# Two exponentials taken from tanh: (1+t)/(1-t) with the quotient on VectorE

## The reference

```python
x = x + conv_ref(ln_c(x), ...)      # deformable convolution, 8 groups, 9 taps
t = t + ffn_ref(ln_t(t), ...)       # 8 experts, the best two of each token
# conv_ref
x1 = gelu(layernorm(depthwise3x3(inputs) + dw_bias))
offset = (x1 @ w_off + b_off).reshape(B, H, W, G, K2, 2)
mask = softmax((x1 @ w_mask + b_mask).reshape(B, H, W, G, K2), axis=-1)
out = sum over the taps of bilinear_sample(x @ w_in + b_in, offset) * mask
return out @ w_out + b_out
# ffn_ref
probs = softmax(xt @ Wr + br); top_p, top_idx = top_k(probs, 2)
weights = top_p / top_p.sum(-1)
y = gelu(layernorm(xt) @ W1[e] + b1[e]) @ W2[e] + b2[e], weighted sum of the two
```

## Time and profile before

| | us |
|---|---|
| median of 3 runs (lowest, highest) | 315.28 (314.25, 315.37) |
| span of the profiled execution, first to last instruction | 312.6 |
| TensorE busy | 278.6 (89%) |
| ScalarE busy | 257.1 (82%) |
| VectorE busy | 240.5 (77%) |
| GpSimd busy | 122.1 (39%) |

### The profile page before, as it was taken

How to read it: one execution, slowest core, us unless ns; L and a number is a source line. 1 busy time by engine, 2 the same in 40 slices (tenths; PEclk the granted TensorE clock), 3 DMA queues, 4 the chain that set the end, 5 groups by cost and what they waited for, 6 DMA issues and landing times.

```text
span 312.6 us, 8542 instructions
## 1 busy us (share of the span) xinstructions
PE 278.6 (89%) x3312; PEld 179.4 (57%) x3312; DVE 240.5 (77%) x720; ACT 257.1 (82%) x495; POOL 122.1 (39%) x123
## 2 busy tenths in 40 slices
PE   7977898968799998899999997999979999998895
PEld 2552476635467654445667663444667787776562
DVE  6999769999957987679878887498958354479565
ACT  3878679899796999989796999988868899887473
POOL 5230151504452705031584413050966713569230
PEclk9999999999999999999999999999999999999999
DMA  6910000000000000000000000000000000000000
GB/s 143 306 37 0 3 2 4 0 2 2 0 3 2 4 2 0 2 0 3 2 9 13 2 0 0 3 2 1 2 19 0 3 2 2 10 1 12 2 0 17
DMA packets 7189, 4.84 MB, mean 15 GB/s; under 512 B 5089, under 2 KB 6830, under 8 KB 7086
## 3 DMA queue, kind: packets, MB, share of 16 engines
q1 hardware_dynamic: 7150, 4.31, 5.7%
HBM read 2.04 MB, written 0.52 MB: 8 GB/s over the span
## 4 chain that ended last, share of the span: by engine, by line
PE 43%; DVE 23%; ACT 18%; issue 9%; POOL 6%; DMA 1%; DVEq 0%; ACTq 0%; POOLq 0%
ACT wk L1284 5%; PE zl_ps L1533 5%; ACT wk L1279 4%; PE ga_ps L1564 3%; PE zh_ps L1530 3%; PE m_ps L1666 3%; PE ga_ps L1566 3%; PE ga_ps L1565 3%; DVE wx L851 3%; DVE prod L863 3%; PE m_ps L1649 2%; ACT h_all L1315 2%; PE m_ps L1507 2%; DVE samp L878 2%; PE m_ps L1452 2%
## 5 line engine op out<-in xcount | busy, mean ns | idle before, releaser
L863 DVE TENSOR_TENSOR prod<-ga_ps,wx 128x480 f32<-128x480 f32 x96 | 61.9, 651 | 30.3 <-PE ga_ps L1566 29.5
L547 POOL TENSOR_TENSOR prod<-prod 128x960 f32<-128x960 f32 (+1 forms) x20 | 39.8, 1991 | 111.6 <-DVE prod L863 111.6
L1279 ACT ACTIVATE wk<-zh_ps 128x512 f16<-128x512 f32 x108 | 65.3, 604 | 21.7 <-PE zh_ps L1530 20.6
L1564 PE MATMUL ga_ps<-v_all,wk 128*128 128x80 f16 x576 | 79.2, 201 | 4.0 <-DVE prod L863 1.4
L1566 PE MATMUL ga_ps<-v_all,wk 128*128 128x80 f16 x576 | 79.2, 202 | 0.0
L1565 PE MATMUL ga_ps<-v_all,wk 128*128 128x80 f16 x576 | 79.1, 201 | 0.0
L1564 PEld LDWEIGHTS ga_ps<-v_all,wk 128*128 128x128 f16 x576 | 56.5, 98 | 17.1 <-issue 6.3
L1284 ACT ACTIVATE wk<-zl_ps 128x512 f16<-128x512 f32 x108 | 65.6, 607 | 0.0
L1565 PEld LDWEIGHTS ga_ps<-v_all,wk 128*128 128x128 f16 x576 | 57.0, 99 | 7.8
L1566 PEld LDWEIGHTS ga_ps<-v_all,wk 128*128 128x128 f16 x576 | 57.2, 99 | 0.0
L1533 PE MATMUL zl_ps<-tab,sel_lo 128*128 128x512 f16 x108 | 41.6, 385 | 7.0 <-ACT wk L1284 4.4
(11 more groups left out here) (283 smaller groups left out, 622.2 us busy)
## 6 DMA issues: line engine op xcount, KB each, us to landing
v_all<-still SPq DMA_DIRECT2D x1, 1440.0 KB, 9.9
h_all<-in_W SPq DMA_DIRECT2D x1, 512.0 KB
w_s<-in_W SPq DMA_DIRECT2D x1, 512.0 KB
x_tok<-in_x SPq DMA_DIRECT2D x1, 384.0 KB, 6.4
out_dram<-x_tok SPq DMA_DIRECT2D x6, 64.0 KB, 1.7
w_high<-w_high SPq DMA_DIRECT2D x1, 256.0 KB, 2.9
const<-in_table SPq DMA_DIRECT2D x1, 218.0 KB, 2.6
vec<-in_vectors SPq DMA_DIRECT2D x1, 132.5 KB
```

Of the source, the lines that this page charges most:

```text
L547: then(pool.tensor_tensor(p[:, 0:3, :], p[:, 0:3, :], p[:, 3:6, :], ALU.add))
L863: dve.tensor_tensor(prod[q % 2][:].rearrange("p k n -> p (k n)")[:, f * PB * NV:(f + 1) * PB * NV] .rearrange("p (n c l) -> p n c l", n=PB ...
L1279: act.activation(wk[n % WR][:, 0, :], zh_ps[:], ACT.Relu, scale=W_SCALE).then_inc(s_wkh, 1)
L1564: pe.matmul(to, w_h, high, start=True, stop=False)
```

## The change

`tap_exp` and `router_exp` on ScalarE take tanh of half the argument, and VectorE computes (1 + t) / (1 - t) in three linked instructions: 1 - t, its reciprocal, and (t + 1) times that. The quotient equals exp of the argument. The three stand at the head of `tap_weights`, for all four chunks, on 128 x 288, and at the head of `expert_weights` for chunks 0 and 1, on 128 x 32. The router of chunks 2 and 3 stays on GpSimd. The warm-up with Exp is gone.

```diff
@@ tap_weights (VectorE)
                 dve.wait_ge(s_ex, a + 1)
                 dve.wait_ge(s_chain, seen["edge"])
+                link(dve.tensor_scalar(below_one[:], th[:], -1.0, 1.0, ALU.mult, ALU.add))
+                link(dve.reciprocal(below_one[:], below_one[:]))
+                link(dve.scalar_tensor_tensor(ex[:], th[:], 1.0, below_one[:], ALU.add, ALU.mult))
@@ expert_weights (VectorE)
                 dve.wait_ge(s_chain, seen["top"])
+                if d < LAST - 1:
+                    link(dve.tensor_scalar(le_below[:], le_th[:], -1.0, 1.0, ALU.mult, ALU.add))
+                    link(dve.reciprocal(le_below[:], le_below[:]))
+                    link(dve.scalar_tensor_tensor(lx[:], le_th[:], 1.0, le_below[:], ALU.add, ALU.mult))
@@ tap_exp (ScalarE)
-                act.activation(ex[:], es[:], ACT.Exp).then_inc(s_ex, 1)
+                act.activation(th[:], es[:], ACT.Tanh, scale=0.5).then_inc(s_ex, 1)
@@ router_exp (ScalarE)
-                act.activation(lx[:, t, :], le[:, t, :], ACT.Exp).then_inc(s_lx, 1)
+                act.activation(le_th[:, t, :], le[:, t, :], ACT.Tanh, scale=0.5).then_inc(s_lx, 1)
@@ before body 0 (ScalarE)
-            act.activation(warm[:, 1:2], still[:, 0:1], ACT.Exp)
```

More of the change, by code:

```diff
@@ L295, in build @@
         mx = sb("mx", [P, TP, Q, 2])
-        warm = sb("warm", [P, 2])
+        warm = sb("warm", [P, 1])
         es = sb("es", [P, TP * S])
         ex = sb("ex", [P, TP * S])
+        th = sb("th", [P, TP * S])
+        below_one = sb("below_one", [P, TP * S])
+        le_th = sb("le_th", [P, TP, E])
+        le_below = sb("le_below", [P, TP, E])
         mask = sb("mask", [P, TP * S])
```

## The result

The changed kernel takes 327.45 us (median of 4 runs, 326.84 to 328.03) against 314.79 us (4 runs, 314.25 to 315.37). The ratio is 1.039, with a 95% interval of 1.036 to 1.042. The forecast was 319.6 us, with a range of 315.0 to 322.5. The sign was right and the time lies 5 us above the range. The profiled execution took 328.02 us, with a span of 326.0 us against 312.6 before.

What follows compares the result with a forecast made beforehand. No engine is full; the chain passes between TensorE, VectorE and ScalarE. Terms 2.83 + 2.73 - 1.1 - 0.2 = +4.3 us on the 315.28 us median gave 319.6 us, range 315.0 to 322.5.

Steps and rivals of the forecast that it cites:

- The price of the passes: Three linked VectorE passes over 128x288 cost 2.83 us a block, with the reciprocal at 1.95 us.
- The table loads: On ScalarE, eight of ten activation-table loads go, leaving two, both at the start.
- Chunk 0 and body 0: VectorE's block stands in the open or in a full stretch: +2.83 us, then +2.83 less 0.1.
- (c): Rival: TensorE's clock falls to 1.2 GHz after the wait before `xn`, 1 to 14 us, taken as 3: 322.6 us; chance 0.08.
- The wait before `xn`: TensorE's wait near the start grows from 0.83 to 3.66 us.
- The warm-up load: Load at 20.8 us, ahead of the chain on VectorE, which does not wait for ScalarE there: worth 0.
- Body 1: ScalarE gives 3.04 us, the block costs 2.83, `feat` had 0.95 of slack: net -1.1 us.
- The loads at 120.9 and 188.3 us lie full on the chain: 1.42 each: In chunks 1 and 2, removing each of these ScalarE loads gains its whole 1.42 us.
- The first load: Load at 109.6 us, priced by its twin without it one chunk later: worth 0.77 us.
- Body 2: ScalarE gives 2.27 us, the block costs 2.83, 0.77 of pause precedes the product at 218.36 us: net -0.2 us.
- (a): Rival: VectorE's block is hidden in bodies 1 and 2 and all ScalarE's gain arrives: +0.25, 315.5 us; chance 0.17.

Runs made afterwards that it cites:

- keep_start: Changed kernel plus 17 matmuls of zeros ahead of TensorE's wait for `xn` of chunk 1; 322.31 us, ratio 1.024.
- two_zeros: Changed kernel plus 2 matmuls of zeros ahead of TensorE's wait for `xn` of chunk 1; 325.75 us, ratio 1.034.
- no_passes: Changed kernel without the VectorE quotients, tanh written where the exponential stood, so the weights are no exponentials; 312.89 us, ratio 0.992.
- delay_start_plus: Kernel before plus unread VectorE pass, reciprocal and two plain passes over 128x288, ahead of chunk 0's weights alone; 323.26 us, ratio 1.021.
- delay_start_double: Kernel before plus unread VectorE passes over 128x288 with two reciprocals, ahead of chunk 0's weights alone; 324.05 us, ratio 1.024.
- pool_newton: Exp kept for chunks 0 and 1; chunks 2 and 3 take tanh with the quotient on GpSimd by Newton steps; 312.94 us, ratio 0.993 against the kernel before.
- exp_first_two: Exp kept for chunks 0 and 1; chunks 2 and 3 take tanh with the quotient on VectorE; 319.14 us, ratio 1.011 against the kernel before.

## Why the prediction was wrong, point by point

The span grew by 13.4 us where 4.3 were summed. Of the 9.1 us between them 6.6 are TensorE's clock, which the sum has at nothing, and 2.5 are ScalarE's gain, which it has too large.

- **The price of the passes: right.** 2.83 us a block was forecast and 2.82 is what each adds between `hats` and `esum`. The slope through two small reciprocals held: 1953 ns against 1.95 us. The Trainium skill ("VectorE: DVE Perf Modes", First, the fixed hardware budget) gives a repeat count of 8 for the divide. The trace disagrees with the estimate of 8.3 ns an element made from it: (1953 - 178) / 284 is 6.25 ns.
- **The table loads: right.** Two are left. The row for GELU of the Trainium skill ("ScalarE: Activation LUTs", Table sets: the hidden batching unit) does not list tanh. The trace goes against keeping the two apart: tanh and GELU alternate there with no load between them.
- **Chunk 0 and body 0, taken as delay: right.** Forecast +2.83 and +2.73, and `keep_start` shows +2.73 and +2.76.
- **The step that failed most: the sum has nothing for the clock, and (c) was mis-weighed.** The wait before `xn` was to become 3.66 us, and the stretch at risk was named, with 1 to 14 us. But it was given 0.08 and 3 us, and the forecast itself goes at full clock. Half clock came in every run of the changed kernel (24 to 27 us of it), and it cost 4.9 us at the start and, by the difference to `keep_start`'s trace, 1.7 us more in bodies 1 and 2 (13.4 - 6.8 - 4.9).
- **The wait itself was 4.08 us and not 3.66.** The warm-up load was put at 0, because VectorE does not wait for ScalarE there. But TensorE does, at its second transposes of `feat`. It comes 0.5 us sooner to the same wait, and 0.83 + 2.75 + 0.5 is 4.08. With the length that was forecast, `two_zeros`' trace has only the short stretch there, and 1.26 us of cost instead of 4.9.
- **Body 1: the other step that failed is "The loads at 120.9 and 188.3 us lie full on the chain: 1.42 each".** The chain led through the load, but TensorE stood just behind it, and all but 0.15 us of the 1.42 came back as a wait. The first load was worth 0.2 us and not 0.77: `es` is late by 0.67 us in `no_passes` where `x2s` was late by 0.86. In all ScalarE gave 1.20 us by `dl` where 3.04 was summed. `keep_start` has 1.53 (5.49 to 3.96). The 0.35 us more come on VectorE at 107.85 us of the kernel before, ahead of the first load, and their cause stays open. The block then adds 2.81, and TensorE's slack before `feat` takes back 1.0, as the forecast's 0.95 said. So body 1 costs +0.3 us instead of giving 1.1.
- **Body 2: the same term.** The gain was 1.0 us and not 2.27, the slack before the product at 218.36 us took back 0.85 against 0.77, and the body costs +1.0 us instead of giving 0.2.
- **The two errors and the range.** Without the clock the sum is 2.73 + 2.76 + 0.3 + 1.0 = 6.8 us, which is what `keep_start`'s span has over before (319.4 against 312.6), against the 4.3 that I gave. This alone would have been 322 us, just inside the range. The clock alone leaves it: 319.6 + 6.6 is 326.2 us. The range ended at 322.5 us, which is (c) at 3 us on the uncorrected sum.
- **(a)** is refuted by `keep_start`'s trace. Of the blocks of bodies 1 and 2, 2.8 us each, only 1.0 and 0.85 us were hidden. What was hidden was more than half of ScalarE's gain.

## What to carry to other kernels

A removed piece that stands on the chain is worth no more than the distance to the next engine behind it (here 0.15 of 1.42 us), so look at what that engine does during the piece before counting its full length. Look also for engines that come sooner to a wait: here a removed load made it 0.5 us longer. When a change lengthens a wait of TensorE ahead of a stretch in which TensorE is the bound, price the wait and, beside it, that stretch at half clock; matmuls of zeros in the wait show which of the two is being paid. An added computation belongs on the engine that has time between its input and its reader: here 13 passes on GpSimd cost less than 3 on VectorE.

## What the runs showed of the hardware

- The granted clock can fall in the middle of a busy kernel. At the wait for `xn` it was 0.50 for 13.6 us behind pauses of 4.1 to 5.6 us in all four traces, for 3.3 us behind 3.6 us in three traces, and behind 2.1 us not at all. But one of four runs of `delay_start_plus` and one of `delay_start_double`, two of those four kernels, had only 5.1 and 7.0 us at half clock in all. Later in the kernel waits of 1.6 to 2.5 us were followed by 3.4 us at half clock, and in `two_zeros` one of 2.44 us by 10.2, so the length of a wait alone does not tell what follows.
- The same program differs between executions by its half clock: `keep_start`'s runs had 3.8 to 24 us of it and took 321.4 to 326.1 us. The mean granted clock explains much of the spread but does not fix the time: the changed kernel's two runs with 27 us at half clock took 326.9 us, and the two with 24 us took 328.0.
- VectorE's reciprocal of 128x288 takes 1953 ns, where plain passes of the same size take 302 and 458 ns.
- VectorE's passes beside GpSimd's in `pool_newton` are longer than the same passes in `exp_first_two`, which makes the quotient on VectorE: 0.34 against 0.17 us for `le_below`, 1.38 against 0.91 us for `dl`.
